# Attention value products of five steps as two 64-row halves into two accumulator banks

## The reference

```
scores = einsum('bhqd,bhkd->bhqk', q, k) / sqrt(16)      # 16 heads, 2048 x 2048
attn   = softmax(scores, axis=-1)
out    = einsum('bhqk,bhkd->bhqd', attn, v)
x      = layernorm(x + out.transpose(0, 3, 2, 1).reshape(b, s, 256) @ Wo + bo)
x      = layernorm(x + (silu(x@w_gate*s_gate) * (x@w_up*s_up)) @ w_down * s_down)
```

## Time and profile before

| | us |
|---|---|
| median of 3 runs | 612.54 |
| lowest, highest | 611.81, 612.61 |
| the profiled execution, its time | 611.91 |
| its span, first to last instruction | 610.1 |
| PE busy, share of the span | 98% |
| ACT busy, share of the span | 84% |
| DVE busy, share of the span | 63% |
| mean granted TensorE clock | 0.994 |

### The profile page before, as it was taken

One profiled execution on the slowest core, in us unless ns is written; L12 is line 12 of the kernel. 1 busy time (PEld: TensorE's weight loads), 2 busy tenths in 40 slices (PEclk: granted clock), 3 DMA queues, 4 the chain that ended last, 5 costly groups with the idle time before them and its releaser, 6 DMA issues.

```text
span 610.1 us, 9962 instructions
## 1 busy us (share of the span) xinstructions
PE 596.8 (98%) x3952; PEld 252.3 (41%) x3952; DVE 386.4 (63%) x508; ACT 510.8 (84%) x586; POOL 55.8 (9%) x51
## 2 busy tenths in 40 slices
PE   8998999999999999999999999999999999999994
PEld 7892222222222323222223232222323226978874
DVE  6672000656666757786875658677757785777875
ACT  4538999999999999999999999999999996253351
POOL 6607000000000000000000000003000001102021
PEclk9998999999999999999999999999999999999998
DMA  9668882211102010101111111112010000101102
GB/s 218 115 102 104 123 113 34 34 26 18 28 11 65 8 31 8 31 7 33 48 28 21 20 22 17 27 12 64 9 32 8 5 5 9 39 0 37 35 0 70
DMA packets 36180, 24.67 MB, mean 40 GB/s; under 512 B 24930, under 2 KB 30946, under 8 KB 35538
## 3 DMA queue, kind: packets, MB, share of 16 engines
q1 hardware_dynamic: 34932, 23.42, 22.5%
q10 hardware_dynamic: 1200, 0.59, 0.4%
HBM read 6.56 MB, written 4.33 MB: 18 GB/s over the span
## 4 chain that ended last, share of the span: by engine, by line
PE 94%; DVE 2%; ACT 1%; DMA 1%; issue 1%; ACTq 0%; POOLq 0%; POOL 0%; DVEq 0%
PE ps L1195 41%; PE ps L1169 30%; PE ps L1300 10%; PE ps L1041 5%; PE ps L1277 4%; PE ps L1217 3%; ACT probs L624 1%; DMA x_tok<-in_L_attn_X 1%; DVE attn_q L779 1%; PE ps L1235 1%; PE ps L1027 1%; DVE stats L983 0%; DVE r_tmp L980 0%; DVE xt_lo L684 0%; DVE r_tmp L977 0%
## 5 line engine op out<-in xcount | busy, mean ns | idle before, releaser
L624 ACT ACTIVATE probs<-ps 128x1024 f32<-128x1024 f32 x484 | 448.3, 1117 | 21.5 <-PE ps L1169 21.5
L1195 PE MATMUL ps<-probs,v_all 128*17 128x512 f32 x1936 | 269.9, 600 | 1.3 <-ACT probs L624 0.3
L1169 PE MATMUL ps<-q_slot,k_stack 51*128 51x512 f32 x1024 | 206.1, 468 | 1.6 <-ACT probs L624 1.6
L1169 PEld LDWEIGHTS ps<-q_slot,k_stack 51*128 51x128 f32 x1024 | 87.7, 184 | 232.7 <-ACT probs L624 219.4
L858 DVE SCALAR_TENSOR_TENSOR poly<-poly,mant 128x1024 f32<-128x1024 f32 x84 | 102.9, 1225 | 2.9
L843 DVE TENSOR_SCALAR bits<-ps 128x1024 int32<-128x1024 f32 x28 | 34.3, 1224 | 72.6 <-PE ps L1169 72.6
L779 DVE COPY attn_q<-ps 128x512 f32<-128x512 f32 x16 | 11.1, 691 | 98.6 <-PE ps L1195 98.6
L643 ACT ACTIVATE sg<-ps,sgate_c 128x512 f32<-128x512 f32 x32 | 22.0, 689 | 49.5 <-PE ps L1300 49.5
L1195 PEld LDWEIGHTS ps<-probs,v_all 128*17 128x17 f32 x1936 | 33.6, 95 | 72.3 <-issue 55.0
L540 POOL TENSOR_TENSOR rstd<-var_eps,minus_half 128x4 f32<-128x4 f32 x4 | 4.1, 1022 | 378.7 <-DVE var_eps L811 378.7
L862 DVE SCALAR_TENSOR_TENSOR poly<-poly,bits 128x1024 f32<-128x1024 f32 x28 | 35.8, 1279 | 2.9
(11 more groups left out here) (95 smaller groups left out, 394.1 us busy)
## 6 DMA issues: line engine op xcount, KB each, us to landing
q_slot<-qy SPq DMA_DIRECT2D x64, 64.0 KB
k_stack<-k_part SPq DMA_DIRECT2D x12, 256.0 KB
at_dram<-attn_q SPq DMA_DIRECT2D x64, 34.0 KB
at<-at_dram SPq DMA_DIRECT2D x8, 272.0 KB, 2.9
q_slot<-qy SPq DMA_DIRECT2D x64, 32.0 KB
x_tok<-in_L_attn_X SPq DMA_DIRECT2D x14, 128.0 KB, 6.0
k_stack<-k_part SPq DMA_DIRECT2D x12, 128.0 KB
out<-out_tmp SPq DMA_DIRECT2D x12, 128.0 KB, 2.4
```

The lines of the kernel that those rows point to most:

```text
L624: nc.scalar.activation(probs[:, n % HALVES, :, :].rearrange("p a b -> p (a b)"), ps[:, 2 * ring:2 * ring + 2, :].rearrange("p a b -> p (a ...
L1169: last = nc.tensor.matmul(ps[:, 2 * ring + half, :], k_stack[s % QUADS][base:base + ROWS, p, kt * P:(kt + 1) * P], q_slot[slot][base:base ...
L1195: last = nc.tensor.matmul(ps[32 * hh:32 * hh + VW, ACC, :], v_all[:, tiles[hh // 2], NQ * (s % QUADS) + hh, :], prob, start=(kt == 0), sto ...
```

## The change

In steps 2, 3, 7, 11 and 15 (`SPLIT`) each value product becomes two: keys 0 to 63 into bank 6, keys 64 to 127 into bank 7. A unit there has eight float32 matmuls of 64 rows for four of 128. `save_attn` of such a step copies bank 6 and then adds bank 7 to the copy, with a wait of DVE on its own copy between (`half_saved`), and only then signals `attn_saved`. The first value product of steps 7, 11 and 15 also waits for `ln1_sum`, the second `ln1_add` of the same step, since bank 7 has held `project_out`'s result. In steps 8 and 12 the first `turn_y` comes after unit 3, where it came after unit 1, since bank 7 holds the sums of the step before until they are saved.

```diff
+    SPLIT = (2, 3, 7, 11, 15)
...
-                nc.vector.tensor_copy(attn_q[s % 2][:], ps[:, ACC, :].rearrange("p (u r) -> p r u", r=HD)
-                                      ).then_inc(attn_saved, 1)
+                halves = [ps[:, ACC + i, :].rearrange("p (u r) -> p r u", r=HD) for i in range(2)]
+                if s in SPLIT:
+                    nc.vector.tensor_copy(attn_q[s % 2][:], halves[0]).then_inc(half_saved, 1)
+                    dve.wait_ge(half_saved, SPLIT.index(s) + 1)
+                    nc.vector.tensor_tensor(attn_q[s % 2][:], attn_q[s % 2][:], halves[1], ALU.add
+                                            ).then_inc(attn_saved, 1)
+                else:
+                    nc.vector.tensor_copy(attn_q[s % 2][:], halves[0]).then_inc(attn_saved, 1)
...
+                if s in SPLIT and s > QUADS and kt == 0:
+
+                    pe.wait_ge(ln1_sum, 2 * (s // QUADS))
...
-                    last = nc.tensor.matmul(ps[32 * hh:32 * hh + VW, ACC, :],
-                                            v_all[:, tiles[hh // 2], NQ * (s % QUADS) + hh, :],
-                                            prob, start=(kt == 0), stop=(kt == TT - 1))
+                    keys = HALF if s in SPLIT else P
+                    for row in range(0, P, keys):
+                        last = nc.tensor.matmul(ps[32 * hh:32 * hh + VW, ACC + row // HALF, :],
+                                                v_all[row:row + keys, tiles[hh // 2], NQ * (s % QUADS) + hh, :],
+                                                prob[row:row + keys, :], start=(kt == 0), stop=(kt == TT - 1))
...
-                if c >= 1 and stage == 0 and kt in (1, 7):
+                if c >= 1 and stage == 0 and kt in (3, 7):
                     turn_y(c - 1, kt // 7)
```

More of the change, by code:

```diff
@@ L212, in layer_program @@
         pv_done = sem("pv_done")
+        half_saved = sem("half_saved")
         attn_saved = sem("attn_saved")
```

## The result

The changed kernel takes 618.85 us (median of 4 runs, 618.18 to 619.99) where before takes 612.56 (4 runs, the three of before the change among them): a ratio of 1.0101, 95% interval 1.0086 to 1.0117, so about 6.3 us slower. Its profiled execution took 618.18, span 616.3.

The account below looks back on a forecast made before the run. ACT was taken to set the pace, PE bounding only at poly tiles. Terms 0.3 + 0.75 + 1.56 + 3.5 = +6.1 us on the 612.54 median gave 618.6, span 616.5 to 621.5 (614.0 to 621.5 with the first rival).

Parts of the forecast that it names:

- What bounds the kernel: Attention units: ACT holds them at 1.81 us, PE alone could do 1.65; PE bounds only for a moment at poly tiles.
- Part 1: Eight half matmuls in split units: 0.03 us longer at each of ten poly places, no drain saved, +0.3 us.
- Part 2: Second half of `save_attn`: `attn_saved` 0.71 us later, costing 0.37 each in steps 3 and 4, +0.75 together.
- Part 3: First value product of steps 7, 11 and 15 waits for `ln1_sum`: +0.52 us each, +1.56 in all.
- Part 4: `turn_y` two units later in steps 8 and 12: 1.75 us each, range 0.93 to 1.9, +3.5 in all.
- Its second half: Steps 8 and 12: DVE reads poly scores behind late transposes; unit 5's second scores wait, 0.75 plus about 0.1 us.
- PE's own half: Steps 8 and 12: PE loses the transposes' cover and waits for `attn_saved`; unit 4 starts 0.93 us later.
- The sum: Whole kernel: 0.3 + 0.75 + 1.56 + 3.5 = +6.1 us, 618.6 on the median.
- No drain within 64 rows: Split blocks: scores and products sharing 64 rows save drains, 0.2 to 0.3 us a block; 614.0 to 614.8, chance 0.13.
- A block shorter by more than its drains: Split blocks: two half-depth streams pass in less than one's 0.44 us; 611.1 us, chance 0.07.
- Slower for lack of concurrency or issue: Split units: a head's halves run one behind the other, +61 us, 673, or PE's issue limits; chance 0.05.
- the first rival: Split blocks: no drain between scores and products in 64 rows; sum +1.4 to +2.3 us, 614.0 to 614.8, chance 0.13.

Follow-up runs that it names:

- e1: Kernel before with only the first `turn_y` of steps 8 and 12 moved from after unit 1 to after unit 3: 615.21 us, ratio 1.0051.
- e2: Changed kernel with only steps 2 and 3 split and `turn_y` back after unit 1: 613.84 us, ratio 1.0026 to before.
- e5: Changed kernel with the second `ln1_add` ahead of `save_attn` in steps 7, 11 and 15: 617.12 us, ratio 1.0080 to before.
- e6: Changed kernel with the first `turn_y` of steps 8 and 12 after unit 2 instead of unit 3: 618.18 us, ratio 1.0090 to before.
- e7: Kernel before with the next unit's first scores ahead of the value products in each step's two poly units: 628.85 us, ratio 1.0254.
- e8: Changed kernel with value products left whole; add, waits and late `turn_y` stay, sums of five steps wrong: 619.28 us, ratio 1.0105 to before.
- e4: Separate program, no waits, score pairs with differently shaped product blocks: per unit 1.65 us whole, 1.67 halves, 1.33 halves of 128 columns.
- e3: Changed kernel without the add of bank 7, half the keys missing from five steps' sums: 618.37 us, ratio 1.0089 to before.

## Why the prediction was right, point by point

**What bounds the kernel.** Right in what mattered: PE has slack in most units and none behind a poly tile, and a delay at a step's start reaches ACT through the start of unit 5. e1, e2, e5 and e6 moved only the steps whose start they touched, by the sizes that this gives. e7 shows where the picture was too simple, since I had not counted the ring.

**Part 1, the half matmuls:** the sign and the reason were right, the size was not. I booked 0.3 (0.03 at ten poly places); changed less e8 is 0.76. The block did get 0.02 to 0.03 longer. But I counted only the block ahead of the unit that sets the gap, and behind a stall three or four blocks lie on the path, in which PE catches up. Step 2, without a stall, shows my 0.06; step 3 shows 0.18, steps 7, 11 and 15 show 0.12 to 0.14, and steps 4, 8 and 12, which I had at nothing, 0.04 or 0.05. That no drain is saved, taken from the earlier trace rows by two changes that were not the one in question, was shown by e4.

**Part 2, the add:** 0.75 for steps 3 and 4; with whole products (e8) 0.36 + 0.38 = 0.74, and without the add (e3) 0.05 and -0.03 are left.

**Part 3, `ln1_sum`:** 1.56; e8 has 1.69 and e5 takes away 1.88, which contains what the longer blocks cost behind the stall. The 0.52 for one step was a little low: the product starts 0.10 after the add, not 0.06.

**Part 4, `turn_y`:** 3.5; e8 has 3.49, the changed kernel 3.58. Its second half, DVE's read of the poly tile behind the late transposes, was the least obvious step; e6 takes exactly that away, 0.82 and 0.81 where I had 0.8. PE's own half was 0.93 forecast, 0.92 in e8 and 0.98 in the changed kernel. For e1 I had expected 1.05 a step and found 1.18, and it is PE's half that was low: 0.37 for 0.22, while DVE's was 0.81 for 0.83. Without the add PE's delay is so short that unit 3 still goes at ACT's pace, 1.80 (281.36 to 283.16), where I took PE's 1.65; in the changed kernel, 0.7 later, it does take 1.65 (283.04 to 284.69).

**The sum:** +6.1 forecast, +6.29 between the medians, +6.63 in steps 2 to 15. The terms that were low are part 1 by 0.46 and part 3 by 0.13. In the traces the clock's grant partly covered that: the changed kernel was 0.68 faster in step 0. The medians differ by less than the steps, too, but step 0 of the runs behind them is not on record. So the closeness of 618.6 to 618.85 is in part luck, by a few tenths.

**The rivals.** No drain within 64 rows: excluded by e4 and by step 2 of e2. A block shorter by more than its drains: excluded by e4, one stream takes the same time with 64 rows. Slower for lack of concurrency or issue: excluded by e4. Two of the sums there were wrong, and neither bears on the forecast: the terms of the first rival add up to +1.7 to +2.5 and not +1.4 to +2.3, and 16 x 0.71 less 0.9 is 10.5 for a step and not 12, so 52 us for five steps and not 61.

## What to carry to other kernels

Before tiles are cut so that they share a shape with their neighbours, look at both rows and columns: here a switch cost about as much whether one or both differed (0.32 to 0.39 us for a pair of switches), and only the block with both alike gained. A second accumulator bank is paid for in the waits of its other users: here 5.9 us of waits against a gain that was 0, with 0.8 us of longer blocks beside them. Most of the waits (3.5) came from moving four transposes two units down PE's list: PE had nothing else to do while DVE copied and added, and DVE's own list waited for the transposes. And where an experiment moves a time by less than the run-to-run clock does, the length of each repeated stretch in the trace resolves what the medians don't.

## What the runs showed of the hardware

- Two changes of shape around a value block cost 0.34 us of PE's pace between 64x128 scores and 64x32 or 64x64 parts (1.67 against 1.33), 0.32 with 128x32 parts (1.65) and 0.39 with 128x128 (1.72), in e4. By the Trainium skill, TensorEngine Tiling (Array Packing), Key Properties, every change of mode drains the engine; e4 agrees for the shapes that it has, and adds the price.
- Eight tiles of 64 rows by 32 columns stream side by side at the pace of four of 128 by 32: 1.67 for 1.65.
- The lengths of steps 2 to 15 repeat within 0.04 us between traces. What else differed between the spans of the traces came, but for 0.1, from their first 76 to 79 us: step 0 took 28.76 at a granted clock of 1.00 (changed), 29.43 at 0.94 (before) and 30.66 at 0.89 (e8).
